# Layer 0 attention: the high parts are written from PSUM by ACT, the low parts by DVE as PSUM minus high

## The reference

```
c_kv = xn @ W_DKV                      # 64 latent features
k, v = c_kv @ W_UK, c_kv @ W_UV        # 16 heads of 16
q    = xn @ W_UQ
scores = q k^T / sqrt(16), causal      # per batch and head, 512 x 512
ctx    = softmax(scores) v
out    = ctx @ W_O
```

## Time and profile before

| | |
|---|---|
| timed runs, median | 2241.44 us |
| profiled execution, its own time | 2235.95 us |
| its span, first to last instruction | 2234.3 us |
| mean granted TensorE clock | 0.895 of 2.4 GHz |
| busy in the span: PE / DVE / ACT / POOL | 1764.3 / 1122.0 / 1024.8 / 1012.5 us |
| layer 0 attention | 0 to about 504 us of the span |
| undisturbed turn of its loop | 54.3 us |

### The profile page before, as it was taken

How to read it: one execution, slowest core, us unless ns; L and a number is a source line. 1 busy time by engine, 2 the same in 40 slices (tenths; PEclk the granted TensorE clock), 3 DMA queues, 4 the chain that set the end, 5 groups by cost and what they waited for, 6 DMA issues and landing times. The chain is left out here.

```text
span 2234.3 us, 33907 instructions
## 1 busy us (share of the span) xinstructions
PE 1764.3 (79%) x10759; PEld 1101.2 (49%) x10759; DVE 1122.0 (50%) x2399; ACT 1024.8 (46%) x1356; POOL 1012.5 (45%) x778
## 2 busy tenths in 40 slices
PE   3888889870599999999999638887887888747933
PEld 2455555540387787787787523333433433235510
DVE  3666666537513313313313148878787787437211
ACT  1455555543313322222223117877787788813400
POOL 3344444320234344343333407777777677724212
PEclk8899999985799999999999858989998999869965
DMA  3333333306201101101100253222222222043999
GB/s 102 87 96 94 94 104 91 94 11 202 84 1 47 47 0 47 47 0 47 45 2 28 77 174 86 67 71 80 80 66 71 81 65 59 10 173 137 345 318 330
DMA packets 129732, 204.38 MB, mean 91 GB/s; under 512 B 14303, under 2 KB 84063, under 8 KB 129668
## 3 DMA queue, kind: packets, MB, share of 16 engines
q1 hardware_dynamic: 107896, 163.40, 24.6%
q10 hardware_dynamic: 16096, 20.65, 2.6%
q0 software_dynamic: 5680, 19.57, 2.2%
HBM read 95.96 MB, written 56.69 MB: 68 GB/s over the span
## 5 line engine op out<-in xcount | busy, mean ns | idle before, releaser
L761 POOL TENSOR_TENSOR l_prob<-l_prob,l_bias 128x1024 f32<-128x1024 f32 x192 | 452.1, 2375 | 149.2 <-ACT l_prob L865 148.4
L1315 POOL TENSOR_TENSOR f_hl<-f_full,f_hh 128x512 fp32r<-128x512 f32 x192 | 247.6, 1290 | 439.9 <-DVE f_hh L1357 283.2
L922 DVE CUSTOM_DVE_ANT_0 l_slot<-l_slot,l_bias 128x512 f32<-128x512 f32 x512 | 340.4, 714 | 52.8 <-PE l_slot L999 51.7
L1357 DVE CAST f_hh<-f_full 128x512 fp32r<-128x512 f32 x128 | 74.8, 585 | 397.7 <-ACT f_full L1336 396.2
L868 ACT ACTIVATE l_prob<-l_prob 128x1024 f32<-128x1024 f32 x256 | 271.1, 1071 | 0.0
L1401 PE MATMUL f_ps<-f_hh,f_hi_h 128*128 128x512 f32 x1024 | 267.1, 397 | 0.0
L1411 PE MATMUL f_ps<-f_hl,f_hi_h 128*128 128x512 f32 x1024 | 265.8, 396 | 0.0
L429 DVE TENSOR_REDUCE l_peak<-l_slot 128x2 f32<-128x256 f32 (+3 forms) x256 | 206.2, 821 | 111.3 <-PE l_slot L526 109.0
L1336 ACT ACTIVATE f_full<-f_ps,f_h_s 128x512 f32<-128x512 f32 x128 | 86.3, 687 | 332.6 <-PE f_ps L1411 308.9
L372 ACT ACTIVATE l_prob<-l_slot 128x1024 f32<-128x1024 f32 (+3 forms) x256 | 174.7, 706 | 96.3 <-PE l_slot L545 93.4
L1401 PEld LDWEIGHTS f_ps<-f_hh,f_hi_h 128*128 128x128 f32 x1024 | 192.8, 188 | 49.3 <-ACT f_hh L1329 2.7
(11 more groups left out here) (209 smaller groups left out, 2691.5 us busy)
## 6 DMA issues: line engine op xcount, KB each, us to landing
l_stacks<-l_parts SPq DMA_DIRECT2D x384, 128.0 KB, 2.7
inter<-e_stage POOLq DMA_DIRECT2D x32, 512.0 KB, 5.1
c_rows<-inter SPq DMA_DIRECT2D x32, 512.0 KB, 9.6
attn<-l_out_sb ACTq DMA_DIRECT2D x16, 512.0 KB, 2.8
f_raw<-in_L_ffn_h_w SPq DMA_DIRECT2D x16, 512.0 KB, 4.2
e_w<-in_L_ffn_f SPq DMA_DIRECT2D x32, 256.0 KB, 4.4
l_bias<-ext ACTq DMA_DIRECT2D x16, 448.0 KB, 11.8
l_x_in<-in_L_attn_x SPq DMA_DIRECT2D x8, 512.0 KB, 3.8
```

Source lines behind the costliest of these rows:

```text
L761: return eng.tensor_tensor(probs(n), src, bias[:, h:h + 2, j * P:j * P + T], ALU.add)
L922: ins = dve.tensor_tensor_reduce(src, src, bias[:, 4 * g + 2 * pr + a, t * P:t * P + T], 1.0, 3 * NEG, ALU.add, ALU.max, peak[:, g, a, pr, ...
L1315: pool.tensor_tensor(hl[layer % 2][:, o], full[:, n % 2], hh[layer % 2][:, o].bitcast(F32), ALU.subtract).then_inc(h_lo.sem, 1)
```

## The change

The three full tiles go, with ACT's copies into them. ACT writes the high part straight from the slot to its fp32r tile. DVE then subtracts the high part from the slot, which is still in PSUM, and writes the low part. POOL does none of the subtractions. The slot is now free when DVE has done the low part (`LAST_READ` names xl_ready, low_ready and ml_ready). The q/k split moves into the step of the qk product itself. The waits that protect the targets (x_saved, stack_in) move from DVE to ACT.

```diff
-                          17: [("mix_turn", -1, 0), ("mix_copy", -1, 0), ("mix_high", -1, 0), ("mix_low", -1, 0)],
+                          17: [("mix_turn", -1, 0)],
-                          12: [("x_turn", 1, 0), ("x_copy", 1, 0), ("x_high", 1, 0), ("x_low", 1, 0)],
+                          12: [("x_turn", 1, 0)],
-                          18: [("qk", 1, 0), ("qk_copy", 1, 0)],
-                          19: [("qk_high", 1, 0), ("qk_low", 1, 0)],
-                          21: [("qk", 1, 1), ("qk_copy", 1, 1)],
-                          22: [("qk_high", 1, 1), ("qk_low", 1, 1)]}.items():
+                          18: [("qk", 1, 0)], 21: [("qk", 1, 1)]}.items():
-        LAST_READ = {"score": a_max, "prob": p_exp, "x_turn": xt_full, "v": v_ready, "qk": qk_copied,
-                     "heads_turn": mix_ready, "mix_turn": mt_full, "out": out_ready}
+        LAST_READ = {"score": a_max, "prob": p_exp, "x_turn": xl_ready, "v": v_ready, "qk": low_ready,
+                     "heads_turn": mix_ready, "mix_turn": ml_ready, "out": out_ready}
 # POOL
-                    if kind == "x_low":
-                        wait(pool, xh_ready, 1, b)
-                        pool.tensor_tensor(xl[:], x_full[:], xh[:].bitcast(F32), ALU.subtract).then_inc(xl_ready.sem, 1)
...
 # ACT (x_turn and mix_turn alike)
-                    if kind == "qk_copy":
+                    if kind == "qk":
+                        for g in (2 * n, 2 * n + 1):
+                            wait(act, stack_in[g], 6, b - 1)
                         wait(act, qk_ps, n + 1, b)
-                        wait(act, low_ready, n, b)
-                        act.copy(qk_full[:], slot("qk", n)[:]).then_inc(qk_copied.sem, 1)
+                        act.copy(parts[:, n, 1:3], slot(kind, n)[:]).then_inc(high_ready.sem, 1)
 # DVE (x_turn and mix_turn alike)
-                    if kind == "qk_high":
-                        for g in (2 * n, 2 * n + 1):
-                            wait(dve, stack_in[g], 6, b - 1)
-                        wait(dve, qk_copied, n + 1, b)
-                        dve.tensor_copy(parts[:, n, 1:3], qk_full[:]).then_inc(high_ready.sem, 1)
+                    if kind == "qk":
+                        wait(dve, high_ready, n + 1, b)
+                        dve.tensor_tensor(parts[:, n, 0:4:3], slot(kind, n)[:], parts[:, n, 1:3].bitcast(F32), ALU.subtract)\
+                           .then_inc(low_ready.sem, 1)
```

More of the change, by code:

```diff
@@ L126, in latent_attention @@
         xh, xl = sb("xh", [P, KD, T], F32R), sb("xl", [P, KD, T], F32R)
-        x_full, qk_full, mix_full = (sb(f"{n}_full", [P, 2, T]) for n in ("x", "qk", "mix"))
         top, cs = sb("top", [P, T], F32R), sb("cs", [P, T], F32R)
@@ L151, in latent_attention @@
         eps_done, rstd_ready = sem("eps_done", 1), sem("rstd_ready", 1)
-        xt_ps, xt_full = sem("xt_ps", 1), sem("xt_full", 1)
+        xt_ps = sem("xt_ps", 1)
         xh_ready, xl_ready = sem("xh_ready", 1), sem("xl_ready", 1)
@@ L155, in latent_attention @@
         v_ps, v_ready = sem("v_ps", 1), sem("v_ready", 1)
-        qk_ps, qk_copied = sem("qk_ps", 2), sem("qk_copied", 2)
+        qk_ps = sem("qk_ps", 2)
         high_ready, low_ready = sem("high_ready", 2), sem("low_ready", 2)
@@ L164, in latent_attention @@
         inv_ready, mix_ready = sem("inv_ready", QUADS), sem("mix_ready", QUADS)
-        mt_ps, mt_full = sem("mt_ps", 1), sem("mt_full", 1)
+        mt_ps = sem("mt_ps", 1)
         mh_ready, ml_ready = sem("mh_ready", 1), sem("ml_ready", 1)
@@ L267, in emit @@
                         sp.dma_start(x_in[:], x_d[b].rearrange("(t p) d -> p t d", p=P)).then_inc(x_loaded.sem, 16)
-                    if kind == "x_low":
+                    if kind == "x_turn":
                         wait(sp, xh_ready, 1, b)
@@ L350, in emit @@
                 def emit(kind, b, n, i):
-                    if kind == "x_copy":
+                    if kind == "x_turn":
+                        wait(act, x_saved, 2, b - 1)
                         wait(act, xt_ps, 1, b)
-                        wait(act, xl_ready, 1, b - 1)
-                        act.copy(x_full[:], slot("x_turn", 0)[:]).then_inc(xt_full.sem, 1)
+                        act.copy(xh[:], slot(kind, 0)[:]).then_inc(xh_ready.sem, 1)
                     if kind == "latent_top":
@@ L377, in emit @@
                         act.copy(o_sb[:, n % 2], o_bank[:]).then_inc(o_copied.sem, 1)
-                    if kind == "mix_copy":
+                    if kind == "mix_turn":
                         wait(act, mt_ps, 1, b)
-                        wait(act, ml_ready, 1, b - 1)
-                        act.copy(mix_full[:], slot("mix_turn", 0)[:]).then_inc(mt_full.sem, 1)
+                        act.copy(mixt[:, 0], slot(kind, 0)[:]).then_inc(mh_ready.sem, 1)
                     if kind == "out":
@@ L409, in emit @@
                                           ALU.subtract, ALU.mult).then_inc(xn_ready.sem, 1)
[L410 to L413, removed]
+                    if kind == "x_turn":
+                        wait(dve, xh_ready, 1, b)
+                        dve.tensor_tensor(xl[:], slot(kind, 0)[:], xh[:].bitcast(F32), ALU.subtract).then_inc(xl_ready.sem, 1)
                     if kind == "latent_low":
@@ L417, in emit @@
                                                  ALU.mult, ALU.add).then_inc(c_ready.sem, 1)
-                    if kind == "qk_high":
-                        for g in (2 * n, 2 * n + 1):
-                            wait(dve, stack_in[g], 6, b - 1)
-                        wait(dve, qk_copied, n + 1, b)
-                        dve.tensor_copy(parts[:, n, 1:3], qk_full[:]).then_inc(high_ready.sem, 1)
-                    if kind == "mix_high":
-                        wait(dve, mt_full, 1, b)
-                        dve.tensor_copy(mixt[:, 0], mix_full[:]).then_inc(mh_ready.sem, 1)
+                    if kind == "qk":
+                        wait(dve, high_ready, n + 1, b)
+                        dve.tensor_tensor(parts[:, n, 0:4:3], slot(kind, n)[:], parts[:, n, 1:3].bitcast(F32), ALU.subtract)\
+                           .then_inc(low_ready.sem, 1)
+                    if kind == "mix_turn":
+                        wait(dve, mh_ready, 1, b)
+                        dve.tensor_tensor(mixt[:, 1], slot(kind, 0)[:], mixt[:, 0].bitcast(F32), ALU.subtract)\
+                           .then_inc(ml_ready.sem, 1)
                     if kind == "score":
```

## The result

The changed kernel takes 2256.3 us (median of five, 2254.40 to 2266.41) against 2241.44 us before (median of five, 2237.09 to 2246.76). The ratio is 1.0078, with a 95% interval of 1.0054 to 1.0101: slower by 0.5 to 1.0%. In the two spans the copy of the last output tile begins at 502.93 us before and at 521.27 us after, so 18.3 of the 18.9 us lie in layer 0's attention.

What follows compares the result with a forecast made beforehand. PE was taken as nearest to a bound, its idle waits and clock deciding. Loop +23.7, ends -5.6 and clock falls +3.3 make +21.4 us on the 2241.44 median: 2262.8, say 2262, range 2248 to 2276.

Steps and rivals of the forecast that it cites:

- The subtraction: DVE's new 128x1024 subtraction from PSUM, taken as 1.22 us from a reduction of the same shape.
- The mechanism: Ring of three PSUM slots: the next use must wait for DVE's subtraction after ACT's pass, with PE there already.
- mix_turn: Turns 1 to 6: the first qk matmul, next user of the slot, starts 1.25 us later.
- qk 0 and 1: The two q/k products: prob 6 starts 1.12 us later, prob 9 1.27, part given back at scores 22 and 23.
- rival (b): Half is repaid as ACT and DVE catch up during stalls: 3.4 a turn becomes 1.7, 2250 us; 15%.
- x_turn: Turns 1 to 6: later release swallowed since value 15's 1.34 us wait for POOL's mask goes; -0.13 us each.
- The ends: Bare chains at the first x and q/k and the last mix_turn: 1.87 us shorter each, together -5.6.
- The clock: PE's clock falling to half after idle stretches: two more falls at 1.65 us each, +3.3 us.
- (a): Faster: slots come free in time, six POOL waits (-8.0) and the bare chains (-5.6) are gained; 2228 us; 7%.
- (c): PE's clock falls at nearly all 13 new idle stretches, 11 more than taken; 2280 us; 12%.
- (d): DVE's subtraction is not 1.22 us: 0.69 gives 2249 us, 2.35 gives 2289; 5%, mostly low.
- (e): No matter: delay and gain cancel by chance within 0.2% or 4.5 us; 2241 us; 6%.

Runs made afterwards that it cites:

- experiment 1: Kernel before, slots of x_turn, qk and mix_turn held until DVE's cast instead of ACT's copy, no instruction changed; 2263.5 us against 2239.4, ratio 1.0108.
- experiment 5: Changed kernel with each split cut into its two PSUM banks, so DVE subtracts one while ACT writes the other; 2243.7 us against 2241.0 before.
- experiment 4: Kernel before with only the mix split done the new way; 2245.0 us against 2239.4, ratio 1.0024.
- experiment 3: Kernel before with only the q/k split done the new way; 2257.4 us against 2239.4, ratio 1.0075.
- experiment 6: Kernel before with POOL's subtraction for x moved one step later, behind the mask of prob 31; 2224.6 us against 2241.0, ratio 0.9913.
- experiment 11: Changed kernel with six extra matmuls, result unused, in front of prob 9 to fill PE's wait; 2263.5 us against 2237.9 before, ratio 1.0089.
- experiment 7: Kernel before, ACT's copies and early release kept, POOL's three subtractions moved to DVE reading SBUF; 2266.2 us against 2241.0, ratio 1.0112.

## Why the prediction was right

The forecast was 2262 (2248 to 2276), the measurement 2256.3. By the steps, from the profiled executions:

- **The subtraction**: 1.22 taken, 1.224 measured.
- **The mechanism** (the slot is held until DVE is done, and PE is there before): shown by experiment 1 without any new instruction, and by experiment 5 with more of them. The prediction gives its ten waits of up to 0.6 us for the copy of q/k to PE's matmuls; the row is one of weight loads (PEld). The matmuls waited five times, 0.34 us, which is what its sum uses.
- **mix_turn**: +1.25 predicted, +1.21 in the undisturbed turn of experiment 4.
- **qk 0 and 1**: 2.15 a turn predicted, 1.79 measured. The two waits came as foreseen: in experiment 3's undisturbed turn the one behind qk 0 is 1.05 (1.12 predicted) and the one behind qk 1 grows from 0.34 to 1.60 (1.27 predicted). What was wrong is what is given back. The 0.42 at score 22 went, as I said. The wait of 0.2 that I then put on for score 23 did not come, and a wait of 0.17 for ACT later in the turn went too. My running sum also has a slip: 3.77 - 0.42 is 3.35 and not 3.2, so added up rightly the term would have been 2.3. It is rival (b) in small, a sixth of the term and not half of the whole.
- **x_turn**: -0.13 predicted, -0.24 measured; by experiment 6 it is +1.22 of release and -1.46 of POOL.
- **The ends**: 1.87 three times predicted. The first score came 3.68 earlier, the last wait before out is 4.34 - 2.45 = 1.89 shorter.
- **The clock**: I added two falls of 1.65, 3.3 us. There were eight in the steady part instead of five, about one a turn, at 1.0 to 1.2 each in experiments 3 and 4. So I had too few falls at too high a price, and that the product came out near 3.3 is luck. The price was too high since I took it from PE's busy time; the turn in the first window of the earlier trace rows, with its two falls, was 2.5 us longer (56.81 against 54.3), 1.25 a fall. The sum fits: 54.32 + 1.21 + 1.79 - 0.24 = 57.1, which experiment 11's turns without a fall confirm (57.15 and 57.17), and one fall of 1.1 makes the 58.2 of the trace. The falls of the changed kernel do stand behind the 1.6 us waits at mix_turn or qk 1, but experiment 11 speaks against these waits as their only cause.
- **The sum**: +21.4 predicted against +18.98 for the profiled executions, +14.9 between the medians. The last 4 us lie between executions: the five runs of each kernel spread over 10 to 12 us, and I carried the 5.5 us between profile and median of before over to after, where the two differ by 1.4 only. That step was weak.

Of the rivals, (a) faster was half right in its gain (removing POOL's wait gives at least the 8 us I gave it: 8.8 by experiment 6's turns, 16 by its medians) and wrong in that slots come free in time. (c) is out with three more falls and not 13, (d) with 1.224 us, and (e) with an interval that keeps clear of 1.

## What to carry to other kernels

Where PSUM slots rotate, price a change of an evacuation by when its last reader ends, not by the busy time of any engine: here 74 us less of POOL bought 5.6 us at the two ends and 1.5 us a turn at value 15, and 1.2 us more of hold cost 1.2 a turn at x_turn and 3 at the other three places. Look for the same loss on the other slots that the same engine frees, as experiment 7 shows. And before an engine is relieved of work, ask whether that work only stands in the wrong place in its queue: moving one subtraction one step gave 16 us by the medians, more than anything else tried here.

## What the runs showed of the hardware

DVE's subtraction of 128x1024 is as fast from PSUM as from two SBUF operands. From PSUM it took 1.224 us. From SBUF, in experiment 7, the means are 1.266 us for q/k, 1.286 for x and 1.375 for mix, but they mix two cases. Where no mask of POOL was in course when it began, it took 1.22 or 1.23 us (as at 250.15). Where one was, it took 1.30 or 1.31, and 1.39 at mix_turn. The groups of that kernel:

```profile
L417 DVE TENSOR_TENSOR l_parts<-l_qk_full,l_parts 128x1024 fp32r<-128x1024 f32 x16 | 20.2, 1266 | 0.6
L405 DVE TENSOR_TENSOR l_xl<-l_x_full,l_xh 128x1024 fp32r<-128x1024 f32 x8 | 10.3, 1286 | 0.3
L424 DVE TENSOR_TENSOR l_mixt<-l_mix_full,l_mixt 128x1024 fp32r<-128x1024 f32 x7 | 9.6, 1375 | 0.2
```

The delay goes the other way too. POOL's masking of 128x256 takes 0.41 us, and in the changed kernel, where these subtractions read the slot and the casts from SBUF are gone, the 256 masks of the attention have a mean of 0.408. In experiment 7 a mask that begins while DVE casts from SBUF took 0.62 or 0.76 us, and one that begins early in a subtraction from SBUF 1.19. These ended 0.26 to 0.28 us behind the DVE instruction beside which they began:

```profile
250.15 1.23 DVE L417 TENSOR_TENSOR l_parts<-l_qk_full,l_parts 128x1024 fp32r<-128x1024 f32 x1
...
256.56 0.76 POOL L312 TENSOR_SCALAR_AFFINE_SELECT l_prob<-l_prob 128x256 f32<-128x256 f32 x1 [4.56 <-ACT l_prob L361]
257.09 1.30 DVE L417 TENSOR_TENSOR l_parts<-l_qk_full,l_parts 128x1024 fp32r<-128x1024 f32 x1
257.48 1.19 POOL L312 TENSOR_SCALAR_AFFINE_SELECT l_prob<-l_prob 128x256 f32<-128x256 f32 x1 [0.16 <-ACT l_prob L361]
```

In the last fence the first mask runs until 257.32, 0.26 us past the end of a cast at 257.06, and the second until 258.67, 0.28 us past the end of the subtraction.

The Trainium skill's table in "VectorE: DVE Perf Modes" (the section on the TRN2 errata) would have a PSUM source cost 62 cycles more. The rows do not show this: 1.224 us from PSUM, 1.22 to 1.23 from SBUF.
